# Roots of the layer norms on ScalarE in groups of tiles, projections ahead of turns, and expert bias products beside the first blocks

## The chip, the cores and the metric

One core of a Trainium2 chip runs the whole program in one launch. The metric is the device time of one execution in microseconds (us). TensorE is called PE in the rows, VectorE DVE, ScalarE ACT, GpSimd POOL and SyncE SP.

## What is computed

A stack of four levels over 64 sequences of 16 tokens, 192 wide, so 1024 tokens. Cut to what matters:

```python
h = tok(x, W, b, pos)                    # patches to tokens
h = h + L0_attn(layernorm(h))            # delays, one head
h = h + L0_ffn(layernorm(h))             # 8 linear experts, top 2, bias
h = h + L1_attn(layernorm(h))            # quantised, 12 heads
h = h + L1_ffn(layernorm(h))             # 4 T5 layers, two with 8 experts, own final norm
h = h + L2_attn(layernorm(h))            # rotary, 12 heads
h = h + L2_ffn(layernorm(h))             # 16 experts, top 2, bias of each expert
h = h + L3_attn(layernorm(h))            # partial rotary
h = h + L3_ffn(layernorm(h))             # 16 experts, top 8
```

`layernorm` subtracts the mean over the 192 columns and multiplies by `1/sqrt(variance + 1e-5)`. The bias of an expert layer is, for each token, the sum over experts of its weight times the expert's output bias.

## The kernel before, in words

The 1024 tokens are 8 tiles (`NT`) of 128 rows, and `h` stays in SBUF. The program is a row of stages (`..._phase`). A stage is one block in which each engine has an instruction stream of its own, written out by hand in loops; the streams wait for each other by counting semaphores, each engine in order, and a barrier of all engines stands between stages (`end_phase`, L181). Nothing reorders the work but the order of these loops. Inside a stage, a loop over steps `s` lets tile `t = s - d` go through its part `d` steps behind tile `s`.

Eight of the nine seams between sub-layers carry a layer norm that runs at the tail of the stage before it. Its parts for tile `t` are:

- VectorE: `bn_stats` and `bn_aggr` give mean and variance (`stats_behind`, L329), the second one step behind the first.
- POOL: `root` (L343) makes `rstd = (var + eps) ** -0.5` with a power, and `offset = -mean * rstd`, three instructions for one tile, each waiting for the one ahead of it.
- ScalarE: `normalise` (L355) writes `h * rstd + offset` to `k.rows`, 256 columns wide: 128 columns, and the other 64 twice, in two instructions; with a `dst` it writes 192 columns in one.
- TensorE: `turn_tile` (L370) transposes both halves of the 256 columns into a bank; ScalarE copies them to `xT` (`keep_tile`, L381); `tile_logits` (L390) multiplies by the router's weights.

The stages that the change touches: `embed_phase` (L221), `out_projection_phase` (L557, POOL adds the bias to `h`, L576), `linear_experts_phase` (L1494), `quant_projection_phase` (L1723, VectorE adds a bias to `h`, L1776), `quant_attention_phase` (L1806), `final_norm_phase` (L400; POOL takes the root of eight tiles' mean squares, L411, then adds to `h`, L416), `compact_attention_phase` (L635, for levels 2 and 3) and `expert_blocks_phase` (L1297, called for 8 experts twice and for 16 experts in level 2).

In `quant_attention_phase` ScalarE's stream has, in step `s`, first `normalise(s - 6)`, then the scores of tile `s` (L1885) and its share of spreading the attention over a block diagonal (L1892). VectorE does the rounding (L1915 to L1927), the context (L1936) and the add to `h` (L1941). POOL rounds the context in three instructions (L1963 to L1967), with `root(s - 5)` ahead of it in the same step.

In `compact_attention_phase` TensorE's step `s` holds scores of tile `s` (behind an idle product, L210, which only keeps TensorE at work), the output projection of tile `s - 4` (L688, one bank, so it waits for the add of the tile ahead, L744), the product with the values of tile `s - 2` (L816), logits of tile `s - 9` and the turn of tile `s - 8`, all turns through one bank.

In `expert_blocks_phase` tokens are sorted by expert into 31 blocks of 128 (23 with 8 experts). POOL fetches rows, weights and sends results by indirect DMA, four blocks ahead. TensorE turns a block's rows (L1368), multiplies (L1380, L1384), and a step later multiplies again (L1396). With `bias`, before the first block, TensorE makes eight products of 16 rows with the biases (L1404) in two banks in turn, and VectorE adds them to `h` (L1462) behind one add over all of `h` (L1459). At the end both rows of a token are brought back, weighted and added, and with `turn_sums` the norm and the turns follow, an idle product behind each turn.

## Time and profile before

| what | us |
|---|---|
| median of 3 runs | 1648.29 |
| lowest, highest | 1633.18, 4505.66 |
| the profiled execution | 1638.03 |
| its span in the profile | 1636.3 |
| embedding | 0 to 35.0 |
| output projection of level 0 | 85.0 to 108.8 |
| linear experts | 120.2 to 173.5 |
| quantised projection, quantised attention | 174.8 to 200.4, 201.3 to 253.1 |
| final norm | 1067.3 to 1088.0 |
| attention of level 2, of level 3 | 1121.4 to 1173.4, 1421.8 to 1475.0 |
| sparse experts of level 2 | 1202.7 to 1388.4 |

The profiled execution's time is 1.7 us above its span, which is what lies around the first and last instruction. The ends of stages are those of their last instruction; some 1.3 us of barrier follow each. A row of the timeline is start, length of the stretch in us, engine, line, operation, written tile <- read tiles, shapes and count; in brackets the idle time of the engine before it and the instruction that ended it. PEclk is the granted clock of TensorE as a share of 2.4 GHz.

### The profile page before, as it was taken

How to read it: one execution, taken by the hardware profiler on the slowest of the kernel's cores; microseconds unless marked ns; L12 is line 12 of the kernel's file. 1: busy time of each engine (PE TensorE's matmuls, PEld its weight loads, DVE VectorE, ACT ScalarE, POOL GpSimd, SP SyncE). 2: the span in 40 equal slices, each digit the busy share in tenths (PEclk: the TensorE clock that was granted, in tenths of full speed). 3: DMA queues.
4: the chain of work that ended last, by engine and by line, in shares of the span. 5: the costliest groups of instructions: out<-in, count | busy, mean ns of one | idle time of the engine just before them, and what ended most of it. 6: DMA issues, size and time to landing. Idle time of an engine off the chain costs nothing. (4 is left out here: it accounts for less than half of the span.)

```text
span 1636.3 us, 35722 instructions
## 1 busy us (share of the span) xinstructions
PE 1381.3 (84%) x14530; PEld 1046.4 (64%) x14530; DVE 591.0 (36%) x1577; ACT 508.8 (31%) x1387; POOL 574.1 (35%) x848
## 2 busy tenths in 40 slices
PE   6669657999998996899999899668569996995997
PEld 4354325888876895688877688624458884362756
DVE  2436562333334212333343411235431112443434
ACT  3330434343441111334343111234313334432120
POOL 2031654222322564323232256454326564350000
PEclk8769858999999998899999899879669998977999
DMA  3100202000003531200000353200044442100000
GB/s 128 39 10 5 97 1 88 3 2 2 12 15 142 176 124 62 90 2 2 2 15 12 150 190 102 91 26 5 27 184 137 165 159 77 37 3 29 30 29 19
DMA packets 40625, 101.96 MB, mean 62 GB/s; under 512 B 15952, under 2 KB 26324, under 8 KB 35344
## 3 DMA queue, kind: packets, MB, share of 16 engines
q0 software_dynamic: 18480, 58.56, 10.4%
q1 hardware_dynamic: 20256, 38.77, 7.0%
q8 instruction: 116, 1.90, 0.5%
q10 hardware_dynamic: 1728, 2.36, 0.5%
q14 instruction: 45, 0.37, 0.1%
HBM read 138.21 MB, written 11.50 MB: 91 GB/s over the span
## 5 line engine op out<-in xcount | busy, mean ns | idle before, releaser
L1396 PE MATMUL bank<-t_ew,t_hg 128*128 128x192 f32 x552 | 97.2, 327 | 0.0
L1433 ACT ACTIVATE t_hg<-bank 128x384 f32<-128x384 f32 x92 | 40.1, 488 | 178.0 <-PE bank L1384 110.1
L2300 POOL TENSOR_SCALAR t_rstd<-t_ssq 128x1 f32<-128x1 f32 x64 | 12.3, 192 | 219.9 <-ACT t_junk L2136 219.7
L1396 PEld LDWEIGHTS bank<-t_ew,t_hg 128*128 128x128 f32 x552 | 88.7, 190 | 0.2
L1708 DVE SCALAR_TENSOR_TENSOR h<-bank,cw,h 128x192 f32<-128x192 f32 x128 | 53.5, 418 | 87.4 <-PE bank L1631 70.3
L1429 ACT ACTIVATE l_hg<-bank,l_ew 128x128 f32<-128x128 f32 x186 | 51.4, 375 | 105.7 <-PE bank L1384 61.5
L1380 PE MATMUL bank<-t_xgT,t_ew 128*128 128x128 f32 x552 | 71.3, 279 | 13.0 <-DVE t_xgT L1474 11.6
L1282 POOL DMA_INDIRECT t_ew<-in_t_moe,source x46 | 47.5, 1033 | 91.0 <-DVE t_og L1483 45.7
L1380 PEld LDWEIGHTS bank<-t_xgT,t_ew 128*128 128x128 f32 x552 | 67.4, 193 | 16.8 <-DVE t_xgT L1474 14.3
L210 PE MATMUL bank<-blk,ident 128*128 128x384 f32 x96 | 49.3, 628 | 32.7 <-issue 19.7
L2057 PE MATMUL bank<-t_wo,t_ctx 128*128 128x192 f32 x384 | 71.0, 335 | 0.9 <-ACT t_ctx L2153 0.9
L366 ACT ACTIVATE rows<-h,offset,rstd 128x128 f32<-128x128 f32 (+1 forms) x96 | 43.7, 496 | 85.5 <-POOL offset L352 84.5
L1631 PEld LDWEIGHTS bank<-w,l_hT 128*128 128x128 f32 x384 | 62.1, 190 | 5.6 <-issue 4.5
L1396 PE MATMUL bank<-l_ew,l_hg 128*128 128x192 f32 x372 | 65.5, 326 | 0.0
L2057 PEld LDWEIGHTS bank<-t_wo,t_ctx 128*128 128x128 f32 x384 | 61.5, 190 | 6.0 <-issue 1.5
L1631 PE MATMUL bank<-w,l_hT 128*128 128x192 f32 x384 | 64.9, 329 | 0.1
L1473 DVE TENSOR_SCALAR t_xgT<-bank,ln2s 128x128 f32<-128x128 f32 x46 | 16.1, 350 | 129.9 <-PE bank L1368 83.2
L1613 PE MATMUL bank<-xT,w 128*128 128x512 f32 x96 | 48.5, 629 | 16.5 <-ACTq L1669 16.5
L2224 DVE TENSOR_SCALAR rows<-z,t_rstd 128x192 f32<-128x192 f32 x64 | 20.5, 320 | 114.6 <-POOL t_rstd L2301 114.6
L1396 PEld LDWEIGHTS bank<-l_ew,l_hg 128*128 128x128 f32 x372 | 59.7, 190 | 0.1
L1340 POOL DMA_INDIRECT rows_out<-t_og,dest x46 | 46.7, 1016 | 31.9 <-DVE t_og L1483 20.2
L1292 POOL DMA_INDIRECT t_xg<-rows_in,token x46 | 44.4, 965 | 36.4 <-DVE t_xgT L1474 19.7
(367 smaller groups left out, 3115.2 us busy)
## 6 DMA issues: line engine op xcount, KB each, us to landing
t_qkv<-in_t_wqkv SPq DMA_DIRECT2D x9, 576.0 KB
t_wo<-in_t_wo SPq DMA_DIRECT2D x8, 576.0 KB
w<-in_l_w SPq DMA_DIRECT2D x8, 576.0 KB, 4.1
wA<-in_t_wqkv SPq DMA_DIRECT2D x2, 1728.0 KB
patches<-in_patches SPq DMA_DIRECT2D x8, 384.0 KB, 5.7
rows_in<-rows SPq DMA_DIRECT2D x24, 128.0 KB, 1.7
t_wi<-in_t_wi SPq DMA_DIRECT2D x3, 576.0 KB
t_gg<-rows_out ACTq DMA_DIRECT2D x8, 192.0 KB, 4.4
```

The source lines that it names most:

```text
L210: pe.matmul(bank[:, 0:HPU * P], k.ident[:], k.blk[:].rearrange("p j q -> p (j q)"), start=True, stop=True)
L366: ins = act.activation(to, x, ACT.Identity, bias=k.offset[:, t:t + 1], scale=k.rstd[:, t:t + 1])
L1282: pool.indirect_dma_start(k.ew[i % W_SLOTS][:, 0:weights.shape[1]], None, weights, bass.IndirectOffsetOnAxis(ap=k.source[:, b:b + 1], axis=0),
L1292: pool.indirect_dma_start(k.xg[i % X_SLOTS][:], None, k.rows_in, bass.IndirectOffsetOnAxis(ap=k.token[:, b:b + 1], axis=0)).then_inc(k.x_l ...
L1340: pool.indirect_dma_start(k.rows_out, bass.IndirectOffsetOnAxis(ap=k.dest[:, own:own + 1], axis=0), k.og[b % O_SLOTS][:], None, bounds_che ...
L1380: pe.matmul(hidden(b, m % 2)[:, m // 2 * P:(m // 2 + 1) * P], w[:, m * P:(m + 1) * P], k.xgT[b % 2][:, 0, :], start=(m < 2), stop=False)
L1396: mm = pe.matmul(k.bank[6 + b % 2][:, 0:DIM], k.hg[b % 2][:, m, :], w[:, SPLIT + m * DIM:SPLIT + (m + 1) * DIM], start=(m == 0), stop=(m = ...
L1429: ins = act.activation(k.hg[b % 2][:, m, :], hidden(b, m % 2)[:, m // 2 * P:(m // 2 + 1) * P], func, bias=k.ew[b % W_SLOTS][:, EXPERT + m: ...
L1613: pe.matmul(pair[o], k.w1[s][:, (m + o) * P:(m + o + 1) * P], k.xTs[:, 0, cols], start=True, stop=False)
L1631: mm = pe.matmul(k.bank[4 + (u * banks + i) % 4][:, j * DIM:(j + 1) * DIM], k.hT[u % 2][:, m, t * P:(t + 1) * P], k.w2[s][:, m, :], start= ...
L1708: ins = dve.scalar_tensor_tensor(out, src, k.cw[:, tile, bass.ds(col, 1)], out, ALU.mult, ALU.add)
L2057: mm = pe.matmul(turn_bank[:, 0:DIM], buf.ctx[w % 2][:, m, :], layer(w).wo[:, m, :], start=(m == 0), stop=(m == FC - 1))
```

## The change

- Groups of tiles: (0, 1), (2, 3), (4, 5), (6), (7). ScalarE takes the square root of variance + eps of a whole group (`deviations`), VectorE the reciprocal, and the offset of the group (`norm_behind`), in six stages. In the embedding and the output projection VectorE normalises itself. In the attentions of levels 2 and 3 the root stays on POOL, by groups. In the final norm the root over all tiles is ScalarE's too.
- Statistics and aggregate of a tile stand in one step, where they were a step apart.
- Only 192 columns are normalised. A turn is two transposes and a product with the identity, which puts the other 64 columns on the second half of the partitions. Where the doubled rows are stored (level 2), ScalarE writes the last 64 again.
- More banks for turns: four in the final norm and the sparse tail, three in the output projection, one and then eight in the attentions.
- In the attentions, the output projections of tiles 6 and 7 stand ahead of the remaining turns and logits, and the logits of tiles 4 to 7 behind all turns.
- In the quantised attention a tile's add stands ahead of the context of a later tile, and the normalisation behind the score work. The quantised projection's bias adds go from VectorE to POOL, a stage earlier.
- Each of the eight bias products stands behind the turn of one of the first eight blocks, in the same bank, and VectorE adds it and the block's tile of `xn` behind the copy of the rows.

```diff
+GROUPS = ((0, 2), (2, 4), (4, 6), (6, 7), (7, 8))
...
+def norm_behind(k, dve, src, done, here=False):
...
+    def step(t):
+        if t < NT:
+            dve.wait_ge(done, t + 1)
+            dve.bn_stats(k.stats[:, t, :], src[:, t, :]).then_inc(k.seen, 1)
+        g = group_ending(t - 1)
+        if g is not None:
+            tiles = slice(*GROUPS[g])
+            dve.wait_ge(k.root_step, g + 1)
+            dve.reciprocal(k.rstd[:, tiles], k.std[:, tiles]).then_inc(k.inverted, 1)
+        if t < NT:
+            dve.wait_ge(k.seen, t + 1)
+            dve.bn_aggr(k.mv[:, t, :], k.stats[:, t, :]).then_inc(k.measured, 1)
+        if g is not None:
+            dve.wait_ge(k.inverted, g + 1)
+            if here:
+                for n in range(*GROUPS[g]):
+                    dve.tensor_scalar(k.xn[:, n, :], src[:, n, :], k.mv[:, n, 0:1], k.rstd[:, n:n + 1], ALU.subtract,
+                                      ALU.mult).then_inc(k.tile_normed, 1)
+            else:
+                dve.scalar_tensor_tensor(k.offset[:, tiles], k.mv[:, tiles, 0], -1.0, k.rstd[:, tiles], ALU.mult,
+                                         ALU.mult).then_inc(k.rooted, 1)
+
+    return step
+
...
+def deviations(k, act, t):
...
+    g = group_ending(t)
+    if g is not None:
+        tiles = slice(*GROUPS[g])
+        act.wait_ge(k.measured, t + 1)
+        act.activation(k.std[:, tiles], k.mv[:, tiles, 1], ACT.Sqrt, bias=k.eps[:, 0:1]).then_inc(k.root_step, 1)
...
+    pool.tensor_scalar(inv, k.mv[:, tiles, 1], 1.0, eps, ALU.mult, ALU.add).then_inc(k.root_step, 1)
+    pool.wait_ge(k.root_step, 2 * g + 1)
+    pool.tensor_tensor(inv, inv, k.power[:, tiles], ALU.pow).then_inc(k.root_step, 1)
+    pool.wait_ge(k.root_step, 2 * g + 2)
+    for n in range(*GROUPS[g]):
+        ins = pool.tensor_scalar(k.offset[:, n:n + 1], k.mv[:, n, 0:1], k.rstd[:, n:n + 1], -1.0, ALU.mult, ALU.mult)
+    ins.then_inc(k.rooted, 1)
...
+    act.wait_ge(k.rooted, GROUP_OF[t] + 1)
+    scales = dict(bias=k.offset[:, t:t + 1], scale=k.rstd[:, t:t + 1])
+    ins = act.activation(dst, src[:, t, :], ACT.Identity, **scales)
+    if doubled:
+        ins = act.activation(k.rows[:, t, DIM:ROW], src[:, t, P:DIM], ACT.Identity, **scales)
...
-    pe.transpose(bank[:, 0:P], k.rows[:, t, 0:P], k.ident[:])
-    pe.transpose(bank[:, P:2 * P], k.rows[:, t, P:ROW], k.ident[:]).then_inc(k.tile_turned, 1)
+    pe.transpose(bank[:, 0:P], k.xn[:, t, 0:P], k.ident[:])
+    pe.transpose(bank[0:REST, P:2 * P], k.xn[:, t, P:DIM], k.ident[:])
+    pe.matmul(bank[REST:P, P:2 * P], k.xn[:, t, P:DIM], k.ident[:], start=True, stop=True).then_inc(k.tile_turned, 1)
```

The embedding's ScalarE and the output projection's POOL:

```diff
-            for s in range(NT + 1):
-                if s < NT:
-                    normalise(k, act, k.h, s, k.xn[:, s, :])
-                t = s - 1
+            act.wait_ge(k.quant_a, 1)
+            for s in range(NT + 4):
+                deviations(k, act, s)
+                t = s - 4
...
         @block.gpsimd
         def _(pool):
-            for s in range(NT + 4):
-                if s < NT:
-                    pool.tensor_tensor(dst[:, s, :], dst[:, s, :], bias[:], ALU.add).then_inc(k.pool_step, 1)
-                if s >= 4:
```

The attentions of levels 2 and 3, TensorE:

```diff
+            for s in range(NT + 2):
                 t = s
...
+                if 4 <= s:
+                    output(s - 4)
...
                     value(pe, t, ptb[t % 2], o_banks(t)).then_inc(k.pv_done, 1)
-                t = s - 9
-                if 0 <= t < NT:
-                    if t == 0:
-                        pe.wait_ge(k.loaded, 16 * len(loads))
-                    tile_logits(k, pe, t, n_e)
-                t = s - 8
-                if 0 <= t < NT:
-                    turn_tile(k, pe, t, (7,))
+                if s == NT + 1:
+                    for t in range(NT - 2, NT):
+                        output(t)
+                if s >= 8:
+                    logits(s - 8)
+                if s >= 7:
+                    turn(s - 7)
+            logits(2)
+            turn(3)
+            logits(3)
+            for t in range(4, NT):
+                turn(t)
+            for t in range(4, NT):
+                logits(t)
```

The sparse experts, TensorE and VectorE:

```diff
+                if bias and 2 <= b < NT + 2:
+                    pe.wait_ge(k.acc_step, b - 1)
                 for c in range(2):
                     mm = pe.transpose(k.bank[b % 2][:, c * P:(c + 1) * P],
                                       k.xg[b % X_SLOTS][:, c * P:(c + 1) * P], k.ident[:])
+                if bias and b < NT:
+                    mm = pe.matmul(k.bank[b % 2][:, 2 * P:2 * P + DIM], k.cwT[0:n_e, b * P:(b + 1) * P], k.bout[0:n_e, :],
+                                   start=True, stop=True)
                 mm.then_inc(k.rows_turned, 1)
...
-            if bias:
-                for t in range(NT):
-                    if t >= 2:
-                        pe.wait_ge(k.acc_step, t - 1)
-                    pe.matmul(k.bank[6 + t % 2][:, 0:DIM], k.cwT[0:n_e, t * P:(t + 1) * P], k.bout[0:n_e, :],
-                              start=True, stop=True).then_inc(k.turned, 1)
-                pe.wait_ge(k.acc_step, NT)
             turn(0)
...
                         dve.tensor_copy(k.xgT[b % 2][:], turned).then_inc(k.rows_copied, 1)
+                    if bias and b < NT:
+                        link(dve.tensor_tensor(dst[:, b, :], k.bank[b % 2][:, 2 * P:2 * P + DIM], dst[:, b, :], ALU.add))
+                        dve.sem_inc(k.acc_step, 1)
+                        link(dve.tensor_tensor(dst[:, b, :], k.xn[:, b, :], dst[:, b, :], ALU.add))
```

The quantised attention, ScalarE and VectorE:

```diff
-            for s in range(NT + 6):
-                t = s - 6
-                if t >= 0:
-                    normalise(k, act, dst, t, k.z[:, t, :])
-                t = s
-                if t >= NT:
-                    continue
+            def behind(s):
+                deviations(k, act, s - 4)
+                if 0 <= s - 6 < NT:
+                    normalise(k, act, dst, s - 6, k.z[:, s - 6, :])
+
+            for t in range(NT):
...
                 ins.then_inc(k.pt_copied, 1)
+                behind(t)
+            for s in range(NT, NT + 6):
+                behind(s)
...
                     ins.then_inc(k.spread, 1)
+                t = s - 3
+                if t >= 0:
+                    dve.wait_ge(k.projected, t + 1)
+                    dve.tensor_tensor(dst[:, t, :], p_bank(t), dst[:, t, :], ALU.add).then_inc(k.added, 1)
                 t = s - 1
                 if 0 <= t < NT:
                     o = k.octx[t % 2]
...
-                t = s - 3
-                if t >= 0:
-                    dve.wait_ge(k.projected, t + 1)
-                    dve.tensor_tensor(dst[:, t, :], p_bank(t), dst[:, t, :], ALU.add).then_inc(k.added, 1)
-                    step(t)
+                if s >= 3:
+                    step(s - 3)
             step(NT)
```

ScalarE's rows in the quantised attention, from tile 5's spreading on (`z` is the normalised tile, `std` the root of a group). Before:

```order
L1892 ACTIVATE attb<-l_xr,unround 32x12x32 x2
L366 ACTIVATE z<-h,offset,rstd 128x192
L1885 ACTIVATE l_xb<-bank,qscale 128x384
L1892 ACTIVATE attb<-l_xr,unround 32x12x32 x2
L366 ACTIVATE z<-h,offset,rstd 128x192
L1885 ACTIVATE l_xb<-bank,qscale 128x384
L1892 ACTIVATE attb<-l_xr,unround 32x12x32 x2
L366 ACTIVATE z<-h,offset,rstd 128x192 x6
```

and with the change:

```order
L1960 ACTIVATE attb<-l_xr,unround 32x12x32 x2
L389 ACTIVATE std<-mv,eps 128x2
L1953 ACTIVATE l_xb<-bank,qscale 128x384
L1960 ACTIVATE attb<-l_xr,unround 32x12x32 x2
L416 ACTIVATE z<-h,offset,rstd 128x192
L1953 ACTIVATE l_xb<-bank,qscale 128x384
L1960 ACTIVATE attb<-l_xr,unround 32x12x32 x2
L389 ACTIVATE std<-mv,eps 128x2
L416 ACTIVATE z<-h,offset,rstd 128x192 x2
L389 ACTIVATE std<-mv,eps 128x2
L416 ACTIVATE z<-h,offset,rstd 128x192
L389 ACTIVATE std<-mv,eps 128x1
L416 ACTIVATE z<-h,offset,rstd 128x192
L389 ACTIVATE std<-mv,eps 128x1
L416 ACTIVATE z<-h,offset,rstd 128x192 x3
```

Each normalisation moved from ahead of a tile's scores to behind its spreading, and five roots came in.

TensorE's rows in the attention of level 3, from the value product of tile 7 on (L816, then L888; `wo` is the projection, `wr` the logits, `ident` the turns). Before:

```order
L816 MATMUL bank<-l_ptb,l_vx 32x32 x48
L396 MATMUL bank<-wr,xT 128x16
L397 MATMUL bank<-wr,xT 128x16
L377 MATMUL bank<-ident,rows 128x128
L378 MATMUL bank<-ident,rows 128x128
L688 MATMUL bank<-l_wo,l_ctxT 128x192 x2
L396 MATMUL bank<-wr,xT 128x16
L397 MATMUL bank<-wr,xT 128x16
L377 MATMUL bank<-ident,rows 128x128
L378 MATMUL bank<-ident,rows 128x128
L688 MATMUL bank<-l_wo,l_ctxT 128x192 x2
```

and with the change:

```order
L888 MATMUL bank<-l_ptb,l_vx 32x32 x48
L729 MATMUL bank<-l_wo,l_ctxT 128x192 x4
L450 MATMUL bank<-wr,xT 128x16
L451 MATMUL bank<-wr,xT 128x16
L430 MATMUL bank<-ident,rows 128x128
L431 MATMUL bank<-ident,rows 64x128
L432 MATMUL bank<-ident,rows 64x128
L450 MATMUL bank<-wr,xT 128x16
L451 MATMUL bank<-wr,xT 128x16
L430 MATMUL bank<-ident,rows 128x128
L431 MATMUL bank<-ident,rows 64x128
L432 MATMUL bank<-ident,rows 64x128
```

The last two projections stand together, ahead of the logits of tile 1, where each was followed by a tile's logits and turn.

TensorE's rows at the head of the sparse experts (`bout` are the biases, `xg` the rows of a block). Before:

```order
L1404 MATMUL bank<-bout,cwT 128x192 x8
L1368 MATMUL bank<-ident,l_xg 128x128 x2
L1380 MATMUL bank<-l_xgT,l_ew 128x128 x6
L1384 MATMUL bank<-l_xgT,l_ew 128x128 x6
L1368 MATMUL bank<-ident,l_xg 128x128 x2
```

and with the change:

```order
L1438 MATMUL bank<-ident,l_xg 128x128 x2
L1441 MATMUL bank<-bout,cwT 128x192
L1453 MATMUL bank<-l_xgT,l_ew 128x128 x6
L1457 MATMUL bank<-l_xgT,l_ew 128x128 x6
L1438 MATMUL bank<-ident,l_xg 128x128 x2
L1441 MATMUL bank<-bout,cwT 128x192
```

The run of eight became one behind each turn.

## Rows read from the trace of the kernel before

**Rows 1.** stretches: start:end, us, busy of PE, PEld, DVE, ACT, POOL, PEclk, DMA, GB/s

```profile
201.30:254.40 53.10, 23.31 (x224) 12.52 (x224) 29.00 (x76) 18.60 (x32) 31.74 (x52) 0.50 0.01 3
1202.60:1389.70 187.10, 162.67 (x1228) 143.96 (x1228) 34.75 (x95) 65.10 (x219) 98.10 (x118) 0.93 0.39 130
1421.70:1476.20 54.50, 48.62 (x1000) 33.28 (x1000) 23.35 (x64) 18.50 (x65) 25.42 (x48) 0.73 0.02 5
```

**Rows 2.** timeline, tail of the linear experts, POOL and ScalarE: start, us, instruction

```profile
168.06 0.19 POOL L348 TENSOR_SCALAR rstd<-mv 128x1 f32<-128x1 f32 x1 [4.35 <-DVE mv L338]
169.34 0.19 POOL L348 TENSOR_SCALAR rstd<-mv 128x1 f32<-128x1 f32 x1
...
173.14 0.38 ACT L1558 ACTIVATE xT<-bank 96x256 f32<-96x256 f32 x1 [0.49 <-PE bank L1515]
```

**Rows 3.** timeline, quantised attention, VectorE, ScalarE, POOL, TensorE

```profile
217.01 0.62 DVE L1915 SCALAR_TENSOR_TENSOR l_xr<-l_xb,rscal,near 128x384 f32<-128x384 f32 x1
220.63 0.60 DVE L1915 SCALAR_TENSOR_TENSOR l_xr<-l_xb,rscal,near 128x384 f32<-128x384 f32 x1
...
227.73 0.55 ACT L366 ACTIVATE z<-h,offset,rstd 128x192 f32<-128x192 f32 x1 [4.36 <-POOL offset L352]
...
243.38 1.07 POOL L1963 TENSOR_SCALAR octx<-octx 128x256 f32<-128x256 f32 x1
...
246.04 1.01 PE L1868 MATMUL bank<-l_wo,l_ctxT 128*128 128x192 f32 x2 [2.04 <-POOL l_ctxT L1967]
...
248.02 0.36 DVE L1941 TENSOR_TENSOR h<-bank,h 128x192 f32<-128x192 f32 x1 [3.28 <-PE bank L1869]
...
252.59 0.55 ACT L366 ACTIVATE z<-h,offset,rstd 128x192 f32<-128x192 f32 x1 [0.73 <-POOL offset L352]
```

**Rows 4.** timeline, embedding, TensorE, VectorE, ScalarE

```profile
16.57 0.31 PE L292 MATMUL bank<-ident,rows 128*128 128x128 f32 x1 [0.89 <-ACT rows L366]
...
27.54 0.36 DVE L322 TENSOR_TENSOR h<-bank,pos 128x192 f32<-128x192 f32 x1 [1.08 <-PE bank L284]
...
34.73 0.26 ACT L236 ACTIVATE xe<-bank 64x128 f32<-64x128 f32 x1
```

**Rows 5.** timeline, output projection, VectorE and TensorE

```profile
95.69 0.36 DVE L627 TENSOR_TENSOR h<-bank,h 128x192 f32<-128x192 f32 x1 [1.74 <-POOL h L576]
...
108.23 0.59 PE L397 MATMUL bank<-wr,xT 64*128 64x8 f32 x2
```

**Rows 6.** timeline, final norm, POOL and TensorE

```profile
1067.98 1.68 POOL L411 TENSOR_TENSOR std<-var,power 128x8 f32<-128x8 f32 x1 [2.76 <-DVE var L428]
...
1075.12 0.47 PE L377 MATMUL bank<-ident,rows 128*128 128x128 f32 x1 [24.27 <-ACT rows L366]
```

**Rows 7.** timeline, sparse experts of level 2, TensorE

```profile
1202.70 1.61 PE L1404 MATMUL bank<-bout,cwT 16*128 16x192 f32 x4 [5.60 <-PEq L183]
...
1209.90 0.69 PE L1368 MATMUL bank<-ident,l_xg 128*128 128x128 f32 x2 [0.45 <-DVE h L1462]
...
1218.68 2.12 PE L1396 MATMUL bank<-l_ew,l_hg 128*128 128x192 f32 x12
...
1223.20 2.12 PE L1396 MATMUL bank<-l_ew,l_hg 128*128 128x192 f32 x12
```

**Rows 8.** timeline, end of that stage, TensorE

```profile
1386.94 1.46 PE L210 MATMUL bank<-blk,ident 128*128 128x384 f32 x4
```

**Rows 9.** timeline, tails of the attentions of levels 2 and 3, TensorE

```profile
1154.80 0.32 PE L688 MATMUL bank<-l_wo,l_ctxT 96*128 96x192 f32 x1 [1.63 <-issue]
...
1461.53 1.48 PE L688 MATMUL bank<-l_wo,l_ctxT 96*128 96x192 f32 x4
...
1474.35 0.61 PE L397 MATMUL bank<-wr,xT 64*128 64x16 f32 x2
```

**Rows 10.** timeline, ScalarE, a table load at the head of a stage

```profile
254.45 1.28 ACT L2136 ACT_TABLE_LOAD   x1 [1.31 <-PEq L183]
255.75 0.36 ACT L2136 ACTIVATE t_junk<-z 128x192 f32<-128x192 f32 x1
```

229 lines of the change are left out of this document (109 added, 120 removed).

## The prediction

> **What bounds the kernel now.** I read the busy time and granted clock of the stages first, then the groups by line, then the timeline engine by engine at the seams between stages, because the chain that ended last only covers the final stage, which the change doesn't touch. The kernel is a row of stages between barriers, so a stage is worth what its own last instruction is late by. The table of stages says which have slack: in the quantised attention no engine is busy more than 31.7 of 53.1 us and the granted clock is 0.50, so it is bound by waits; in the last attention TensorE is busy 48.6 of 54.5 us at 0.73; in the sparse expert stage 162.7 of 187.1 [rows 1]. The waits in question are those for the root: each of 64 tiles (8 in each of eight stages) has three POOL instructions of its own, among them the power, and one root starts 1.28 us behind the other (168.06, 169.34) [rows 2]. Where eight tiles arrive faster than that, the tail of the stage is POOL's.
>
> **The change part by part.** Times are against the profiled execution: span 1636.3 us, 1638.0 us on the clock of the runs, so 1.7 lie around it. The median of the three runs is 1648.3, but with two at 1633.2 and 1648.3 I hold 1638.0 for the centre.
>
> Quantised attention. ScalarE stood 4.36 us before tile 0's normalisation, which is ahead of tile 6's scores in its program, and as long again before tile 1's: POOL reached the root only behind a whole context step. VectorE's tile steps start 3.62 apart until then (217.01, 220.63) [rows 3]. Now ScalarE takes a root for two tiles behind its own spreading, and the normalisation stands behind the tile's score work, so both stalls go. VectorE gets earlier statistics, a reciprocal and an offset, 0.15 to 0.2 each, 1.1 in the three tile steps that matter. Step 7 ends near 220.6 + 3 x 3.6 + 1.1 = 232.6. The end of the stage is now VectorE's new order: the add of tile 5 before the context of tile 7, so that context leaves at about 235.1; POOL takes 2.66 to pass it on (243.38 to 246.04), the projection 1.98 (246.04 to 248.02) [rows 3], which is 239.8; statistics, root, reciprocal and offset 1.2 to 1.4, three normalisations of 0.45 in a row, end 242.5. Before it was 252.59 + 0.55 = 253.1. Gain 10.5; bounds 8 (one more step of 3.6 lost in part) and 12 (no reorder cost).
>
> Embedding. TensorE waited 0.89 for tile 0's normalisation and needn't now. From the last add (27.54) to the end (34.99) there are 7.45 us [rows 4]. Now statistics, root and aggregate take 1.2, and ScalarE then works off the copies of five tiles at 0.65 each: 4.4. Gain 0.9 + 3.0 = 3.9; bounds 2 and 5.
>
> Output projection. POOL's bias add is queued behind a root, and VectorE waits 1.74 for it; the same happens for the next two tiles through TensorE. The stage ends at 108.8 [rows 5]. With the eight adds in one run (0.6 each from 85.0) there is no such wait. VectorE now normalises itself and becomes the bound: add, statistics, aggregate, half a reciprocal, normalisation, 1.25 a tile from tile 3 at 93, 99.5 at the last. Then turns and logits of the last three tiles, 1.4 each warm and 1.85 cold: 104.3. Gain 4.5; bounds 2 and 6.
>
> Linear experts. TensorE bounds the loop and stays so; the tail takes three roots in a row from 168.06 and ends at 173.5 [rows 2]. Now tiles 6 and 7 alone are left behind the last add, with roots of 0.2: 170.9. Gain 2.6; bounds 1.5 and 3.5. The bias adds, gone from VectorE's quantised projection to POOL here, are 0.6 each beside free time; the projection ends with POOL anyway, gain 0.4, bounds 0 and 1.
>
> Final norm. The power of eight columns took 1.68; a root and a reciprocal do it in 1.1 from the barrier, the 1.28 of a table load being most of it. TensorE starts at 1075.12 with the first turn [rows 6] and would start at 1073.3. Its work grows, since a turn is now three products and not two: 0.4 a tile cold, 0.2 warm. Gain 1.4; bounds -0.5 and 3.
>
> Sparse experts, head. TensorE and VectorE spend 1202.70 to 1209.90, 7.2 us, on eight bias products before the first block turns [rows 7]. Now each stands behind the turn of one of the first eight blocks: 0.33 warm, 0.75 the first. A block takes 4.53 (1218.68, 1223.20 [rows 7]), and VectorE's two more adds (0.8) lie under TensorE's second product. 7.2 - 0.75 - 7 x 0.33 = 4.1; some blocks wait for fetched rows anyway and may swallow part, so I take 4.3; bounds 1 (the first blocks run cold twice as long) and 7.
>
> Sparse experts, tail. It ends at 1388.4 [rows 8]. The first turn would come 0.75 earlier, but TensorE's idle products bound the rest, and the third product of a turn costs it 0.4 a tile cold. Gain 0.5; bounds -1 and 2.
>
> Attentions of levels 2 and 3. Roots stay on POOL for pairs, and cost 1.4 a pair. The last projection ran from 1461.53 and would run from about 1459.9. But it is now followed by seven logits and six turns instead of six and five: 7 x 1.07 + 6 x 0.95 + 0.9 of waits = 14.1, where 12.2 were spent before until 1474.96 [rows 9]. Nothing is won there while the clock is at 1.2 GHz; at 2.4 GHz the same work is 8. In level 2 TensorE stood 1.63 without work shown before 1154.80 [rows 9], which may have cost the clock; I take 3.0 for level 2 and 0.8 for level 3; bounds for both together -2 and 11.
>
> Table loads. Six more: three at the head of a stage, where the first use is over a microsecond off, three before a root. The row shows 1.28 and the next ScalarE instruction 0.02 behind it [rows 10]; where it stands in mid-stream (output projection, sparse tail) the root's inputs are not ready 0.9 us of it. I count 0.5 in all, which the terms above hold already. The Trainium skill ("ScalarE: Activation LUTs", What ACT_TABLE_LOAD costs) says that a switch is 1.28 us of load and 1.38 us of drain. The load agrees with the row; no drain shows here, but these rows have nothing in flight before them. By the page the two mid-stream switches and the final norm would cost 1.4 each more, and the sum would be 4 less.
>
> Sum: 10.5 + 3.9 + 4.5 + 2.6 + 0.4 + 1.4 + 4.3 + 0.5 + 3.8 = 31.9, no overlap since each lies in its own stage. 1638.0 - 31.9 = 1606, or 1.95%. A measurement of this kernel tells about 2%, 32.8 us, from no change, so the forecast stands on that line, a hair below.
>
> **The rivals.**
> A. The clock carries the attentions. If TensorE keeps 2.4 GHz through the tails of both, they end 4 to 5 us earlier each than taken, and the embedding and output tails lie at their upper bound: 1606 - 9 - 2 = 1595. For it: TensorE is denser with the projections back to back. Against it: it was at 1.2 GHz in both tails before, busy four fifths of the time [rows 9].
> B. The tails are given back. VectorE becomes the bound where it normalises, every root is a round trip VectorE, ScalarE, VectorE behind in-order queues, and drains are paid at the switches. Each of the six tails gives half its gain: 0.5 x (3.9 + 4.5 + 2.6 + 1.4) = 6, the quantised attention is at its lower bound, 2.5, the attentions give nothing, 3.8, and switches 2: 1606 + 14 = 1620. For it: the added waits stand in queues, ScalarE's root of a pair before the copies of earlier tiles in the embedding and the output projection.
> C. Slower. The sparse experts become bound by their fetches. Four blocks are in flight, a block is 4.53 us, and some waits of 1.8 us show already. If the bias work on VectorE delays each block's copy and so POOL's next fetch, the 27 fetched blocks all wait 1.8: 49 us, less the 27.6 of the other stages: 1638 + 21 = 1659. It decides from the point where a fetch takes longer than three blocks. Against it: the DMA engines are busy 0.39 in that stage [rows 1], and only eight blocks carry the extra work.
> D. The change doesn't do what it says: an in-order queue locks the new order into the old one in the quantised attention (the root of a pair waits for an aggregate that waits for the score work). Then 10.5 is lost: 1616. Against it: the aggregate of tile 1 stands a whole step before the root that reads it.
>
> **How the numbers follow.** Forecast (gain 25 to 40) 0.55; A 0.13; B 0.19; C 0.03; D 0.10. The runs of before spread over 15 us, which lies on both sides of each. From 1592 to 1628 leaves out half of A's far side, C and a little of B: about 0.15 to 0.2. Faster by over 2% needs 32.8: half of the forecast's 0.55 and all of A: 0.40. Slower by over 2% is part of C alone: 0.02. Within 2%: 0.58.
>
> **What would show it.** Right: no idle time of ScalarE over 1 us before a normalisation in the quantised attention, and that stage about 42 us and not 53; the first block's turn within 1 us of the barrier; first blocks 4.9 apart; the output projection some 19 us long. The tail of the level 3 attention after its last projection 14 us long at the low clock would confirm that it wins nothing, 9 that A holds. Wrong: ScalarE waiting long for an aggregate, VectorE for a root; 1.4 us of nothing before a table load; block distances over 6 for most blocks.

## The result and the profile after

The changed kernel takes 1634.5 us (median of 20 executions, 1623.1 to 1644.9), the kernel before in the same comparison 1644.2 (20 executions, 1632.3 to 1653.0 but for one of 4505.7). The ratio is 0.9946, with a 95% interval of 0.9925 to 0.9967: a gain of half a per cent, some 9 us, where I had forecast 31.9. A second comparison (chip 11; twelve executions of the changed kernel, 29 of the one before) gives 0.997 (0.9937 to 1.0002). Neither is a difference of 2%, and 1606 with its range of 1592 to 1628 was wrong. Some 6 us of the distance from 1606 to 1634.5 lie in the base alone: I took 1638.0 for the kernel before, and its median is 1644.2.

The stages tell more than the sum. These are rows of the changed kernel's profile by stretches (length; busy us and count of TensorE, its weight loads, VectorE, ScalarE, POOL; the granted clock as a share of full; DMA share; GB/s), in the order: quantised attention, the first and the second pair stage of the T5 layers, attention of level 2, sparse experts of level 2, attention of level 3.

```profile
195.00:237.30 42.30, 23.01 (x224) 12.35 (x224) 30.96 (x86) 19.44 (x37) 23.73 (x28) 0.51 0.01 3
237.30:487.30 250.00, 242.33 (x3806) 196.55 (x3806) 90.00 (x203) 98.25 (x300) 72.23 (x133) 0.97 0.06 21
645.80:897.40 251.60, 240.43 (x3806) 195.02 (x3806) 89.99 (x203) 98.24 (x300) 72.39 (x133) 0.98 0.06 21
1112.60:1168.80 56.20, 49.68 (x1016) 31.81 (x1016) 24.89 (x64) 18.23 (x65) 23.60 (x42) 0.81 0.08 24
1196.90:1380.90 184.00, 163.75 (x1244) 143.91 (x1244) 36.78 (x112) 64.78 (x217) 89.91 (x94) 0.96 0.39 132
1412.90:1469.20 56.30, 51.61 (x1016) 33.44 (x1016) 24.89 (x64) 15.70 (x57) 23.58 (x42) 0.75 0.02 5
```

The first, fifth and sixth answer to [rows 1] (53.1, 187.1, 54.5). The quantised attention won what was forecast. The last attention got longer by 1.8 us, with 16 matmuls more and 3 us more of TensorE's time. And the two T5 stages, which the change doesn't touch, have the same 3806 matmuls as before but are longer: in the first profile of before they were 245.2 and 248.8 us.

Every stage from its start to the next one's start, before minus after (a gain is positive), for the first profiles of both kernels (the one of before is that of the prediction) and for a second pair from the second comparison. Lines are rounded each for itself:

| stages | predicted | first pair | second pair |
|---|---|---|---|
| quantised attention | 10.5 | 10.9 | 10.8 |
| embedding | 3.9 | 2.6 | 3.1 |
| output projection | 4.5 | 3.6 | 2.5 |
| linear experts | 2.6 | 2.8 | 2.9 |
| quantised projection | 0.4 | -0.6 | -0.5 |
| final norm | 1.4 | 0.6 | -0.1 |
| sparse experts of level 2, head and tail | 4.8 | 3.1 | -0.1 |
| attentions of levels 2 and 3 | 3.8 | -4.6 | -11.6 |
| the two T5 pair stages | 0 | -7.8 | -11.0 |
| level 0 attention | 0 | -1.6 | -0.1 |
| all others | 0 | -2.9 | 1.1 |
| sum | 31.9 | 6.0 | -3.0 |

So some 20 us came in the four stages whose waits went, where 21.5 were forecast. Most of it was paid back in other stages. One profile has a luck of its own: the second one of before was faster (1609.6 us) than all 29 other executions of that kernel in its comparison (1612.6 to 1639.3), so the second column flatters the kernel before, and the ratios, not these sums, say what the change is worth. The table is for finding the places. One line of it is not the change's: the 1.6 us of the level 0 attention are 3.4 us at 1.2 GHz at the head of that stage, which the other three profiles don't have.

Two places in the trace show what was paid. The first is TensorE's timeline in the tail of the level 2 attention, behind its last projection: one turn (lines 430, 431, 432) and the first product of the next.

```profile
1160.64 0.48 PE L430 MATMUL bank<-ident,rows 128*128 128x128 f32 x1
1160.91 0.42 PE L431 MATMUL bank<-ident,rows 128*64 128x128 f32 x1
1161.26 0.69 PE L432 MATMUL bank<-ident,rows 128*64 128x128 f32 x2
1161.88 0.48 PE L430 MATMUL bank<-ident,rows 128*128 128x128 f32 x1
```

A turn takes 1.24 us (1160.64 to 1161.88). The third product is one line but "x2": it has two matmul records (two passes, I call them), where a transpose has one. The tail, from the end of the last projection to the last logits, is 15.74 us long in both attentions; before it was 11.94.

The second is in the untouched T5 stage, TensorE's timeline in the products of the probabilities with the values (line 2177), 96 tiny ones in a row:

```profile
451.95 0.88 PE L2162 MATMUL bank<-t_kx,t_qT 128*32 128x64 f32 x48
452.76 1.14 PE L2177 MATMUL bank<-t_ptb,t_v 32*64 32x32 f32 x92
455.03 0.30 PE L2177 MATMUL bank<-t_ptb,t_v 32*64 32x32 f32 x4 [1.14 <-issue]
```

After 92 of them TensorE stands for 1.14 us "on issue", in the middle of a row of equal products that wait for nothing. I numbered TensorE's instructions in the trace (weight loads, matmuls and those of its sequencer): this place is number 8642, the other such place of the stage (1792 or 7 times 256 earlier) number 6850, and in the second T5 stage, a second pass over the same code, numbers 16692 and 18484, again 1792 apart. The page lists a queue that carries TensorE's program (packets, MB, share of the DMA engines' time):

```profile
q8 instruction: 117, 1.92, 0.5%
```

117 loads of 16 KB for 29,936 instructions, 256 to a load. The instructions that the change adds ahead of this stage (32 in the output projection, less one) moved every later one, and so moved which of them is the first of a load. The Trainium skill ("Runtime: NRT & Kernel Launch", Instruction fetch mechanics) says that an engine's program comes in blocks of 16 KiB, 256 instructions, and that crossing into the next is mostly hidden. The trace agrees on the block and its size; that it is hidden holds at most boundaries here, and not at these.

The times of these loads are in the trace, and they settle what TensorE waits for. The load ahead of number 8642 landed at 453.60 and TensorE went on at 455.03, 1.43 us later; ahead of number 6850 the two are 400.86 and 402.12, 1.26 apart. In the fourteen profiles of this study, the T5 stages and the attentions of levels 2 and 3 hold 77 pauses of 0.45 us or more at such a number, and 76 of them end 1.2 to 1.6 us after a load has landed; of the boundaries that TensorE passed without a pause (0.15 us or less), 9 in 100 lie in such a place by chance.

The kernel before has them too. Its boundaries have the same numbers, but other products stand there (line 2021, 128x128): 0.41 us at 8642 and at 18484 in its first profile, 0.28 at 6850 in its second. And [rows 9] shows one that I read without knowing it: the 1.63 us "on issue" before 1154.80 in the attention of level 2 are at number 23348, which is 23604 less 256; that load landed at 1153.33, 1.47 us before TensorE went on.

### The profile page after: what moved, and what is told of

The parts are those of the page before. It is cut to its first block and busy times, and to the rows that moved or that the text cites. A ratio compares the mean times of both kernels' runs of the same rounds, so it can differ in the third digit from the quotient of the medians.

```text
span 1630.2 us, 35793 instructions
## 1 busy us (share of the span) xinstructions
PE 1398.5 (86%) x14610; PEld 1054.0 (65%) x14610; DVE 606.6 (37%) x1644; ACT 503.9 (31%) x1376; POOL 524.6 (32%) x699
## 5 line engine op out<-in xcount | busy, mean ns | idle before, releaser
L1453 PE MATMUL bank<-t_xgT,t_ew 128*128 128x128 f32 x552 | 72.7, 283 | 14.3 <-DVE t_xgT L1534 13.3
L1453 PEld LDWEIGHTS bank<-t_xgT,t_ew 128*128 128x128 f32 x552 | 68.3, 196 | 18.6 <-DVE t_xgT L1534 16.7
L211 PE MATMUL bank<-blk,ident 128*128 128x384 f32 x96 | 46.9, 600 | 28.7 <-issue 18.2
L1469 PEld LDWEIGHTS bank<-l_ew,l_hg 128*128 128x128 f32 x372 | 59.7, 190 | 1.5 <-issue 1.4
L1413 POOL DMA_INDIRECT rows_out<-t_og,dest x46 | 46.7, 1016 | 33.5 <-DVE t_og L1547 21.9
L1453 PE MATMUL bank<-l_xgT,l_ew 128*128 128x128 f32 x372 | 48.5, 281 | 7.7 <-DVE l_xgT L1537 7.7
```

The lines of the kernel that those rows point to most:

```text
L211: pe.matmul(bank[:, 0:HPU * P], k.ident[:], k.blk[:].rearrange("p j q -> p (j q)"), start=True, stop=True)
L1413: pool.indirect_dma_start(k.rows_out, bass.IndirectOffsetOnAxis(ap=k.dest[:, own:own + 1], axis=0), k.og[b % O_SLOTS][:], None, bounds_che ...
L1453: pe.matmul(hidden(b, m % 2)[:, m // 2 * P:(m // 2 + 1) * P], w[:, m * P:(m + 1) * P], k.xgT[b % 2][:, 0, :], start=(m < 2), stop=False)
L1469: mm = pe.matmul(k.bank[6 + b % 2][:, 0:DIM], k.hg[b % 2][:, m, :], w[:, SPLIT + m * DIM:SPLIT + (m + 1) * DIM], start=(m == 0), stop=(m = ...
```

## The experiments

The theory: (1) the third product of a turn costs two passes, in every turn behind the final norm, the attentions and the sparse experts; (2) more instructions on TensorE's queue move its program loads to places where they are late, and a late load can take the clock with it; (3) the rest is as predicted. Rivals: chance of single executions, the time at which the clock rises above all; the attentions' new order; the parts other than the quantised attention give nothing for reasons of their own.

### Both kernels again

No edit; the kernel before, once, and the changed kernel in twelve executions.

> The kernel before, unchanged, once more, for its stages. My theory: the stage lengths of the first profile are properties of the program, so the first relative-position (T5) stage is again 243.9 + 1 us from its first to its last instruction, the second 247.4, the attentions of levels 2 and 3 53.4 and 54.5 from start to the router's start, and TensorE has no stall inside a row of products at 0.8 us or over in the T5 stages. Rival (chance): the T5 stages differ from the first profile by 3 us or more.

> The changed kernel, unchanged, once more. My theory: it is some 0.5% faster than the kernel before (ratio 0.993 to 0.997); the T5 stages are again 4.9 and 2.9 us longer than before's, with the same two stalls of TensorE inside the products on the value tiles (0.3 and 1.1 us, 89 and 59 products in), and the attentions of levels 2 and 3 take 56.2 us each. Rival (chance): the T5 stages come out at before's 243.9 and 247.4.

Measured: the T5 stages came to 245.3 and 247.6 us in the kernel before, without a stall of 0.3 us inside a row, and to 249.9 and 253.9 in the changed one, with stalls at numbers 6850 and 8642 (0.42 and 0.86 us) and at 16692 and 18484 (0.59 and 0.82). The places are the program's; the sizes vary. Chance as the only cause of the T5 loss is out, as the stalls are there again; but the lengths have a share of it: the clock rose 6.6 us into the second T5 stage in the kernel before and 16.7 us into it in the changed one, and, as the runs below show, the same code has it at either. But I was wrong on the attentions of the kernel before: 50.1 and 49.8 us, not 53.4 and 54.5.

```profile
1108.80:1158.90 50.10, 43.65 (x1000) 28.46 (x1000) 23.30 (x64) 18.24 (x65) 25.34 (x48) 0.84 0.09 26
1187.40:1365.50 178.10, 161.41 (x1228) 144.30 (x1228) 35.08 (x95) 64.95 (x219) 97.71 (x117) 0.93 0.41 136
1397.60:1447.50 49.90, 43.12 (x1000) 28.61 (x1000) 23.36 (x65) 18.24 (x65) 25.36 (x48) 0.85 0.02 5
```

Against [rows 1]: the same attention of level 3 at a granted clock of 0.85 in place of 0.73 is 4.6 us shorter, and the changed kernel has 57.9 and 53.7 here. But this is the fastest execution of the kernel before. Over six profiles with this very code in the attentions they take 49.8 to 56.1 us, 53.4 in the mean, so the row that I built the term on (54.5) was an ordinary one, and a single pair tells little. The sparse experts took 178.1 us and not 187.1, again with the same code. In the first profile a block took 5.1 to 6.1 us ten times, in pairs every fourth or fifth block, here nearly all take 4.53. The changed kernel has such blocks in its first profile too (up to 6.03 us) and none in its second; these pauses come and go between comparisons and executions, and nothing I ran tells their cause.

### Moving TensorE's program, first try: waits

In the delay stage, where TensorE does nothing:

```diff
+        @block.tensor
+        def _(pe):
+            for _ in range(448):
+                pe.wait_ge(k.evacuated_a, 1)
```

> The changed kernel with 226 instructions more on TensorE's queue, all waits that are already met, in the delay stage where TensorE has nothing to do. They move every later TensorE instruction by 226 places, which with the 31 that the change added by the T5 stages makes about one whole load of the program (16 KB, 256 instructions). My theory: the stalls of TensorE come at fixed places of its instruction stream (those of the two profiles all stand at the same number modulo 256 within a pass), where the next 16 KB of program have not arrived; so the T5 stages lose their stalls of 1.1 us and the clock drop behind the first, and come back to some 245.5 and 247.5 us (before 243.9 and 247.4, plus the later rise of the clock in the first). 5 to 6 us less than the changed kernel, ratio to before 0.990 to 0.992. Rival (the stalls belong to what the engines compute there, or to chance): the T5 stages stay at 248.8 and 250.2, the ratio at 0.995.

Measured: ratio 1.0007 (0.9972 to 1.0043), slower than the changed kernel alone. By stretches, the delay stage and the first T5 stage:

```profile
32.50:60.30 27.80, 0.00 (x0) 0.00 (x0) 12.34 (x10) 11.09 (x10) 0.00 (x0) 0.50 0.17 45
243.40:488.60 245.20, 238.57 (x3806) 193.35 (x3806) 90.00 (x203) 98.37 (x300) 72.23 (x133) 0.99 0.06 21
```

The T5 stage is at 245.2 as forecast, the length it had before the change; one stall of 0.38 us is left in it. Part of that is the clock, which rose 4.3 us into the stage here and 9.3 in the changed kernel's run. The 448 waits are 224 instructions in the trace, two waits in each, and a met one takes TensorE 0.11 us, so they took 24 us and made the delay stage 10.1 us longer. And TensorE stood 2.32 us in the attention of level 2, at number 23604: its loads had moved, too. The second T5 stage, at 252.7, wasn't what I expected: its clock rose only 13.3 us in, and stalls of 0.32 and 0.43 us are left.

### The same with tiny transposes

```diff
+            for _ in range(112):
+                pe.transpose(k.bank[7][0:32, 0:32], k.ident[0:32, 0:32], k.ident[0:32, 0:32])
```

> The changed kernel with 225 TensorE instructions more in the delay stage, now as 112 tiny transposes of 32x32 in place of waits (the 226 waits took 10.1 us of their own in the run before and hid what they gave). My theory: the delay stage stays at 17.7 us within 1; the first T5 stage falls from 249.9 to 245 to 246 with no stall of 0.8 us or more inside a row of products, the second keeps the later rise of the clock at its head and loses 1 to 2 us; in the attention of level 2 a stall of about 2 us remains, at another product. In all 3 to 6 us under the changed kernel, ratio to before 0.991 to 0.995. Rival (places in the program don't matter): 0.997, T5 stages at 250 and 252.

Measured: 0.9954 (0.9928 to 0.998). The stretches: delay stage, both T5 stages, attention of level 2.

```profile
33.90:51.60 17.70, 6.13 (x112) 6.00 (x112) 12.34 (x10) 11.09 (x10) 0.00 (x0) 0.50 0.28 70
237.90:484.40 246.50, 240.33 (x3806) 194.98 (x3806) 89.98 (x203) 98.28 (x300) 72.02 (x133) 0.98 0.06 21
636.60:886.60 250.00, 239.45 (x3806) 194.61 (x3806) 89.98 (x203) 98.29 (x300) 72.16 (x133) 0.98 0.06 21
1095.60:1155.70 60.10, 53.62 (x1016) 34.39 (x1016) 24.89 (x64) 18.24 (x65) 23.54 (x42) 0.74 0.07 22
```

The shift is free now, and the T5 stages win 3.3 and 3.9 us on the changed kernel's 249.9 and 253.9. Of these the 3.3 are a clean comparison: in both profiles the clock rises 9.4 us into the first stage, and the one difference is two stalls of together 1.28 us and 3.4 us at 1.2 GHz behind them. The 3.9 are not, since the clock rises 6.9 us into the second stage here and 16.7 there; one stall of 0.68 us is left in it (number 18228). The attention of level 2 is at 60.1, with a stall of 2.05 us at number 23604. What the shift wins in one stage it loses in the next, unless it is chosen for both. By the ratio alone it is not to be told from the changed kernel (0.9946 and 0.997).

### Before's attentions in the changed kernel

The functions of before for the attentions of levels 2 and 3 (order, single roots, two-product turns); all else changed.

> The changed kernel with the attentions of levels 2 and 3 as before: roots of single tiles, projections behind the turns, turns of two products on doubled rows. My theory: these two stages go back from 56.2 and 56.3 us to 53.4 and 54.5, which is 4.6 us less, ratio to before 0.990 to 0.993; the sparse experts and the hidden stage stay within 1 us. Rival 1 (the attentions lost by chance of the clock or of program loads, not by their new order): they stay at 55 or more. Rival 2 (other stages take it back): the attentions fall but the sum does not.

Measured: 0.9938 (0.9909 to 0.9968), where the changed kernel in the same comparison had 0.997. The stages were 54.8 and 54.0 us, after 57.9 and 53.7. The level 3 one holds a stall of 1.71 us at number 28468, which the kernel before doesn't have there. So the attentions may be some 0.3% of the loss, but the intervals overlap, and the ratios don't show it.

### Two-product turns, order kept

```diff
-    pe.transpose(bank[0:REST, P:2 * P], k.xn[:, t, P:DIM], k.ident[:])
-    pe.matmul(bank[REST:P, P:2 * P], k.xn[:, t, P:DIM], k.ident[:], start=True, stop=True).then_inc(k.tile_turned, 1)
+    pe.transpose(bank[:, P:2 * P], k.rows[:, t, P:ROW], k.ident[:]).then_inc(k.tile_turned, 1)
...
-                normalise(k, act, dst, t, k.xn[:, t, :], doubled=keep)
+                normalise(k, act, dst, t, k.xn[:, t, :], doubled=True)
```

in the final norm, the attentions of levels 2 and 3 and the sparse experts' tail.

> The changed kernel with its order kept, but every turn in the final norm, in the attentions of levels 2 and 3 and in the tail of the sparse experts made of two products on rows that ScalarE has doubled, as before, in place of three, the third of which TensorE runs in two passes (0.35 us each at 1.2 GHz). My theory: a turn at the low clock falls from 1.24 to 0.7 us; the attentions of levels 2 and 3 fall by 2 to 5 us each from 57.9 and 53.7, the final norm and the tail by 1 to 2 each; ratio to before 0.988 to 0.993. Rival 1 (the attentions lose by the order, with projections ahead of all turns, and by the clock that falls in it): less than 1.5 us each, the tail stays 16 us long. Rival 2 (ScalarE becomes the bound with a second part for every tile): final norm and tail grow.

Measured: 0.9885 (0.9842 to 0.9929), a median of 1603.7 us where the kernel with tiny transposes above, in the same comparison, has 1613.9. TensorE's timeline in the same tail as above:

```profile
1149.59 0.42 PE L688 MATMUL bank<-ident,rows 128*128 128x128 f32 x1
1149.81 0.42 PE L689 MATMUL bank<-ident,rows 128*128 128x128 f32 x1
1150.02 0.42 PE L688 MATMUL bank<-ident,rows 128*128 128x128 f32 x1
```

A turn is 0.43 us at the low clock where it was 1.24, and the tail is 11.14 us and not 15.74. The final norm fell by 3.1 us (22.2 to 19.1) and the sparse experts by 3.8 (178.2 to 174.5). The tail of 16 us of rival 1 and the growing stages of rival 2 are out: the order alone doesn't make the tail long, and ScalarE has room for the second part. But the attentions as a whole are 55.0 and 54.4, the first 2.9 shorter and the second not shorter at all, where I expected 2 to 5 each; each has a stall at a program load again, 2.31 and 2.02 us.

### The mirror: the third product alone, in the kernel before

```diff
-    pe.transpose(bank[:, P:2 * P], k.rows[:, t, P:ROW], k.ident[:]).then_inc(k.tile_turned, 1)
+    pe.transpose(bank[0:REST, P:2 * P], k.rows[:, t, P:DIM], k.ident[:])
+    pe.matmul(bank[REST:P, P:2 * P], k.rows[:, t, P:DIM], k.ident[:], start=True, stop=True).then_inc(k.tile_turned, 1)
```

> The kernel before with one thing alone: a turn is three products (the second half of a tile turned twice, once as a product into the lower partitions) where it was two; the rows are still doubled by ScalarE as before, and nothing else is touched. It is the mirror of turn2all. My theory: the third product is two passes, 0.57 us a tile at the low clock; the tails of the attentions behind the last projection go from 11.9 to 15 to 16.5 us, the final norm and the sparse experts' tail grow by 2 to 4 us each, the output projection by 0 to 3; in all 10 to 15 us slower, ratio to before 1.006 to 1.010, the mirror of the 0.85% that turn2all gives back. Rival (turn2all gained by chance of the clock or by fewer program loads): 1.000 to 1.003, tails of 12 to 13 us.

Measured: 1.0149 (1.0109 to 1.0189), 23 us slower by the medians (1645.6 and 1622.6), more than I expected. The stretches: output projection, both T5 stages, attention of level 2; and the timeline of the first T5 stage in the values' products.

```profile
84.20:113.10 28.90, 24.78 (x112) 18.31 (x112) 5.67 (x24) 12.11 (x32) 12.49 (x32) 0.73 0.00 1
257.00:505.20 248.20, 240.34 (x3806) 194.96 (x3806) 89.95 (x203) 98.26 (x300) 72.22 (x133) 0.98 0.06 21
658.10:911.50 253.40, 242.27 (x3806) 196.56 (x3806) 89.94 (x203) 98.28 (x300) 72.36 (x133) 0.97 0.06 21
1117.50:1177.20 59.70, 53.17 (x1016) 34.26 (x1016) 23.52 (x64) 18.27 (x65) 25.45 (x48) 0.73 0.07 22
```

```profile
471.16 1.14 PE L2112 MATMUL bank<-t_ptb,t_v 32*64 32x32 f32 x92
472.89 0.30 PE L2112 MATMUL bank<-t_ptb,t_v 32*64 32x32 f32 x4 [0.59 <-issue]
```

The eight third products of the output projection are 32 more TensorE instructions (a weight load and a matmul for each pass, and two passes), the same 32 as in the changed kernel. With them alone the stalls are at 6850, 8642, 16692 and 18484 inside the values' products, after the 92nd of 96 at number 8642 as above, and larger than the kernel before has them at these numbers (0.5 to 1.0 us); the T5 stages are at 248.2 and 253.4, though the clock of the second, which rose 13.1 us in, has its share. This joins the two halves of the theory: one cause, a third product per turn, costs its passes where it stands and program loads where it doesn't. The attentions went to 59.7 and 59.8 (tails 15.04, where the same order with two products has 11.94), the output projection up by 3.8, final norm and sparse experts by only 1.0 and 1.7.

### Idle products ahead of the T5 stage

In both profiles of the changed kernel the clock rose 9.3 to 9.4 us into the first T5 stage, in both of the kernel before 4.3 to 4.4. I took that for the change's doing.

```diff
+            idle_products(pe, k, k.bank[0], 5)
```

behind the last projection of the quantised attention.

> The changed kernel with five idle products (0.7 us each at 1.2 GHz) behind TensorE's last projection of the quantised attention, where it otherwise has nothing to do for 4 us until the barrier. My theory: the first T5 stage loses 1.6 us because the clock there rises 9.3 us after the stage's start and not 4.1 as before; with TensorE busy up to the barrier the clock rises within 5 us of the start, the stage is 1 to 2 us shorter than 249.9, and the quantised attention's own 42.3 us stay within 0.3. Ratio to before 0.995 to 0.998 (about 0.1% under the changed kernel's, less than a ratio tells; the stage decides). Rival (the rise has nothing to do with the idle time before): the clock rises 9 us in again and the stage stays at 249.9.

Measured: 0.9976 (0.9946 to 1.0006). The two stages:

```profile
195.50:240.10 44.60, 28.02 (x234) 14.95 (x234) 30.95 (x86) 19.43 (x37) 23.69 (x28) 0.54 0.01 3
240.10:487.50 247.40, 238.40 (x3806) 193.76 (x3806) 89.99 (x203) 98.16 (x300) 72.01 (x133) 0.99 0.06 21
```

The clock was up before the T5 stage began, which won 2.5 us with the stalls as before (0.40 and 1.05). But the five products took 5.0 us and not 3.5 (each is two records again) and ended behind the normalisations, and the quantised attention grew by 2.3. The lever is real and was worth nothing as I pulled it. Nor is the late rise the change's: the kernels with before's attentions and with two-product turns run the same TensorE code up to here and have the rise at 4.3 and 5.1 us.

### Two-product turns and a shift chosen for them

From the traces I worked out, for each shift, how long TensorE takes over each stretch of 256 instructions in the T5 stages and the new attentions. At 227 more, none is shorter than 2.5 us. The edit is the kernel with two-product turns and 113 tiny transposes in the delay stage. Beside it ran the same with the attentions as before the change and a shift of its own.

> The kernel of turn2all (two products a turn behind the final norm, the new attentions and the sparse experts) with 227 TensorE instructions more in the delay stage, 113 tiny transposes. At 227 places on, no stretch of 256 instructions of the T5 stages or of the new attentions is issued in under 2.5 us (worked out from the start times in the traces so far). My theory: the stalls inside rows of products, 2.8 us in the T5 stages and 4.3 in the two attentions of turn2all, fall under 1 us in all, the clock stays up in more of the tails, the first T5 stage is 245 to 246, the attentions 50 to 53 each; 5 to 9 us less than turn2all, ratio to before 0.981 to 0.986. Rival (the stalls were other things' and come back at new places): 0.9885 again, stalls of 2 us in the attentions.

> The same with the attentions of levels 2 and 3 as before the change (projections behind turns, root for each tile), and the shift chosen for them (169 in the delay stage, 32 in the final norm). It compares the two orders of these attentions with two-product turns in both and few stalls in either. My theory: the new order gives and takes nothing much; the two stages come to 50 to 53 us in both kernels and differ by less than 1.5 each. Rival 1 (the order ahead of the turns is a loss, since the tail runs at the low clock): this kernel's attentions are 3 us or more shorter each. Rival 2 (the order is a gain of 2 us each once the turns are cheap): they are longer by that.

Measured: 0.9824 (0.9787 to 0.9862), a median of 1598.8 against 1622.9, the fastest kernel of this study; its interval lies on both sides of a gain of 2%. Its T5 stages and attentions:

```profile
241.00:486.30 245.30, 238.93 (x3806) 193.37 (x3806) 89.91 (x203) 98.27 (x300) 71.99 (x133) 0.99 0.06 21
641.40:889.90 248.50, 238.79 (x3806) 193.35 (x3806) 89.91 (x203) 98.26 (x300) 72.16 (x133) 0.99 0.06 21
1096.00:1150.30 54.30, 47.79 (x1000) 32.73 (x1000) 24.91 (x64) 18.33 (x65) 23.56 (x42) 0.75 0.08 25
1386.70:1440.70 54.00, 48.14 (x1000) 32.68 (x1000) 24.87 (x64) 18.22 (x65) 23.54 (x42) 0.75 0.02 5
```

Inside rows of products of the T5 stages no stall over 0.2 us is left, in the attentions one of 0.27. But between rows two are left there, ahead of a turn in level 2 (number 23604) and at a projection in level 3 (1.00 us, number 28468); they end 1.4 and 1.5 us after a load has landed. The first:

```profile
1131.02 0.45 PE L688 MATMUL bank<-ident,rows 128*128 128x128 f32 x1 [1.85 <-issue]
```

The 256 instructions ahead of it had taken 3.4 us, so the 2.5 us that I chose the shift by are no bound. The attentions stay at 54, with these stalls and with the clock low for their last 20 and 17 us; my 50 to 53 was wrong. The kernel with before's attentions had 0.9893 (0.9849 to 0.9936) and 55.7 and 56.2 us, but its shift was chosen badly (stalls of 2.12 and 1.56 us are in it). So which order is better for these attentions isn't settled: the new one is not a loss of 3 us, and no gain of it is shown. The two kernels' medians in this comparison, 1598.8 and 1606.7, differ by more than the attentions do.

### One part alone: the quantised attention

Kernel before, with only that stage's new code.

> The kernel before with one part of the change alone: the quantised attention with ScalarE's roots for groups behind its spreading and with VectorE's new order. TensorE's program keeps its length, so that the places of its program loads stay as before. My theory: that stage goes from 53.1 to 42.3 us as in the whole change, the first T5 stage keeps 245 us (no stall of over 0.3 us inside a row of products) or pays 1 to 2 us for a later rise of the clock, and all else stays; 9 to 11 us less, ratio to before 0.993 to 0.995. So this part alone gives as much as the whole change (0.995 and 0.997). Rival (the other parts give their share too and this one less than the stage shows): 0.997 or above.

Measured: 0.9946 (0.9927 to 0.9965), the ratio that the whole change had in the first comparison (0.997 in the second). Its stage and the T5 stage behind it:

```profile
201.10:244.80 43.70, 23.31 (x224) 12.52 (x224) 30.94 (x86) 20.71 (x38) 23.69 (x28) 0.50 0.01 3
244.80:491.10 246.30, 239.84 (x3806) 194.79 (x3806) 89.92 (x203) 98.26 (x300) 72.01 (x133) 0.99 0.06 21
```

43.7 and not 42.3: ScalarE has one instruction more (x38), since the table load falls into this stage (in the whole change it has been done ahead). So all other parts of the change together came to nothing that these intervals can tell. TensorE's program is untouched here, yet the second T5 stage took 252.5 us from barrier to barrier, 3.4 to 4.5 more than in the kernel before's two profiles: its clock rose 13.2 us in. Not all of the T5 stages' loss in the table is thus the change's.

### One part alone: the experts' bias

Kernel before, with only the bias products moved beside the first eight blocks.

> The kernel before with the part on the sparse experts' bias alone: no eight products ahead, one beside the turn of each of the first eight blocks. My theory: the first output copy comes 4.5 us earlier than before's 18.2 to 18.6 after the stage's start, five of the distances behind it are 5.23 and not 4.53 (a product of fp32 is two passes of 0.35 us) and the whole stage is 1.0 to 1.5 us shorter, not 4.3 as predicted; ratio to before 0.998 to 1.000, no difference that can be told. Rival (the distances in the profiles of the changed kernel came from something else, the tail's three-product turns or the places of program loads): distances of 4.9 or 4.53 and a stage 4 us shorter.

Measured: 1.0007 (0.9988 to 1.0026). VectorE's first two output copies of the sparse experts:

```profile
1213.23 0.36 DVE L1479 COPY l_og<-bank 128x192 f32<-128x192 f32 x1 [3.02 <-PE bank L1401]
1218.11 0.36 DVE L1479 COPY l_og<-bank 128x192 f32<-128x192 f32 x1 [1.01 <-PE bank L1401]
```

The stage starts at 1194.0, so the first copy comes 19.2 us in, later than before's 18.2 to 18.6 and not 4.5 earlier. The following distances are 4.9, 5.2, 5.2, 5.2 and 5.2 us as forecast. The rival is out. What went wrong is the clock at the head:

```profile
1194.00:1212.20 18.20, 17.01 (x70) 13.71 (x71) 3.14 (x9) 4.59 (x13) 0.94 (x1) 0.50 0.15 51
```

It was at 0.50, which is 1.2 GHz, for 18 us, with TensorE 17.0 us busy. In the changed kernel's first profile it rose 5.5 us in and the first copy came at 13.2. Where the clock rises late, real blocks run through the low clock in place of the short bias products. It is no trait of this kernel alone: of the ten profiles with the bias work beside the blocks, eight have the rise 5.4 to 7.5 us in and the first copy at 13.2 to 14.2; this one and the one with idle products have the rise at 18.3 and 18.1 and the copy at 19.2 and 18.7. In the four with before's head it rises 11.3 to 12.7 us in. So the part wins 4 to 5 us at the head in most profiles and lost 0.6 in this one, and a single profile doesn't price it; what decides isn't shown.

## Why the prediction was wrong

The forecast's mechanism for the main term held. The quantised attention is 42.3 us, forecast "about 42": the score work follows without ScalarE's stall, and the last add starts 38.4 us into the stage (233.40 less 195.0), where before it was 46.7 (248.02 [rows 3] less 201.3). With it rival D is out. One sign that I had named for being wrong did come and meant nothing: ScalarE waits up to 2.2 us for an aggregate in the tail, but the adds set the pace there. The linear experts are right within 0.3 us. Embedding and output projection gave 2.6 to 3.1 and 2.5 to 3.6, inside their bounds of 2 to 5 and 2 to 6, but 1 to 2 us below the values taken; where the clock is low in the output projection's last 7 us (both profiles with two-product turns and the new order) only 0.7 to 0.8 is left of the latter. The table loads are right as I took them: in mid-stream of the output projection ScalarE ends a copy, loads, and takes the root with nothing between.

```profile
88.26 0.38 ACT L661 ACTIVATE l_ctxT<-bank 96x256 f32<-96x256 f32 x1 [1.33 <-PE bank L636]
88.66 1.28 ACT L389 ACT_TABLE_LOAD   x1
89.95 0.30 ACT L389 ACTIVATE std<-mv,eps 128x2 f32<-128x2 f32 x1
```

The drain of 1.38 us of the Trainium skill ("ScalarE: Activation LUTs", What ACT_TABLE_LOAD costs) doesn't show here: 0.02 us stand between the copy and the load.

The step that failed is the price of the turn: "a turn is now three products and not two: 0.4 a tile cold, 0.2 warm". Measured against the tiles of the tails, a turn went from 0.43 (0.48 in [rows 9]'s own tails) to 1.24 us at the low clock, 0.8 more. The tails of the attentions, forecast at 14.1 us with six turns at 0.95, were 15.7, for which six turns at 1.24 account, and not the 11.9 of before; with the third product gone they are 11.1. In two terms the price, too low as it was, wasn't even added: for the final norm I took 1.8 us of earlier start less 0.4, where eight turns at my own 0.2 are 1.6, and for the sparse tail a gain of 0.5, where eight at 0.4 are 3.2. They came to 0.6 and -0.1 for the norm and to a loss of 0.3 and 1.3 for the tail. The trace of before had the price, in a stage I read for another reason: the embedding turns its tiles with the same kind of product, here at the low clock.

```profile
30.16 0.47 PE L292 MATMUL bank<-ident,rows 128*128 128x128 f32 x1 [1.82 <-ACT rows L366]
30.56 0.69 PE L293 MATMUL bank<-ident,rows 128*64 128x128 f32 x2
```

The bias product fell to the same error. [rows 7] has four matmuls in 1.61 us for two products at the low clock. I took 0.33 a product at the high one; the changed kernel's row there shows two matmuls and 0.59:

```profile
1217.82 0.59 PE L1441 MATMUL bank<-bout,cwT 16*128 16x192 f32 x2
```

Five of the distances between blocks grew by 0.70 (5.23 and not 4.53), where I had 4.9 in mind. In the second pair, with the first copy 4.4 us earlier (18.6 to 14.2) and 3.5 given back over the distances, 0.9 of the 4.3 is left, and the tail took that back.

The second failure is a term I didn't have: what a change does to stages that it doesn't touch. "No overlap since each lies in its own stage" was the sentence. The T5 stages lost 7.8 and 11.0 us in the two pairs. For the first stage the parts are shown: the stalls at program loads, with the clock that fell behind them, are 3.3 us (249.9 against 246.6 with the loads moved and the same late rise), and the later rise of the clock at the head is 1 to 2 (4.3 and 9.4 us in). The stalls are the program's and the rise is the execution's. The fall of the clock within a stage goes with the stalls: in the T5 stages of all fourteen profiles it fell fifteen times for some 3.4 us, each time 0.2 to 2.0 us behind the end of a pause at a program load, and never elsewhere; behind rather more than half of these pauses it didn't fall. In the second stage the rise, 16.7 us in against 6.6, is about half of the second pair's loss by an estimate: 9.4 us at the low clock at the head cost 2.5 in the first stage (249.9 against 247.4 with idle products ahead), so 10 more cost some 3. All profiles together, from barrier to barrier:

| TensorE's program in the T5 stages | profiles | first stage, mean | second stage, mean |
|---|---|---|---|
| as before the change | 4 | 245.2 to 247.1, 246.0 | 248.0 to 252.5, 250.2 |
| third product in the output projection, not shifted | 6 | 246.1 to 250.1, 248.4 | 251.4 to 257.4, 253.5 |
| the same, shifted | 4 | 245.3 to 246.6, 245.7 | 248.9 to 253.1, 250.6 |

So the change costs these two stages 5 to 6 us in the mean, and not 7.8 or 11.0, and a shift gives it back.

The third is the 3.0 us that I took for level 2, on the ground that a gap of 1.63 us would go and the clock stay up. The gap was a program load; the changed kernel has two there (0.84 and 1.31 us, numbers 23348 and 23604), and the clock was low for the last 17.6 us of the stage, where it was for 18.2 before. With the clock these stages vary by 6 us for the same code, so single pairs mislead here as well:

| code of the attentions of levels 2 and 3 | profiles | us | mean |
|---|---|---|---|
| before's order, two products a turn | 6 | 49.8 to 56.1 | 53.4 |
| before's order, three products | 1 | 59.7, 59.7 | 59.7 |
| new order, three products | 5 | 52.8 to 60.0 | 56.7 |
| new order, two products | 2 | 54.0 to 55.0 | 54.4 |

By the means the changed kernel loses 3.3 us a stage here, 2.3 of it by the third product.

Rivals: A didn't come, since the clock stays low in both tails (only in the second profile's level 3 was a part of it at the high one, and it took 13.6 us). B's 1620 was nearest to the number, but not for its reasons: the tails with new roots kept most of their gain, and what was given back went to the third product. C is out: behind the first eight the blocks stand 4.53 us apart in the second pair, and in the first pair both kernels have the same longer ones. The forecast of 1.95% isn't far from what the change gives once its turns have two products and its loads are placed: 1.76%. That doesn't make it right, as the changed kernel has neither.

## What to carry to other kernels

Count passes, not products: before pricing a matmul that replaces a transpose, find a row of the same kind in the trace and look at its count beside its time. Where an engine issues hundreds of tiny instructions in a row, adding instructions anywhere ahead of them can move a program load into that row; compare the untouched stages first when a gain goes missing, and number the engine's instructions at their "issue" stalls. Take a stage's length from several executions before building a term on it or reading a loss from it: the same attention code took 49.8 to 56.1 us, and the fastest execution misleads as much as a slow one. And add each price that you name to every term that pays it.

## What was unexpected of the hardware

- TensorE's program loads of 16 KB can be late: stalls of 0.3 to 1.1 us in the T5 stages, up to 2.3 in the attentions, at the same numbers of the stream for the same program. Where the 256 instructions ahead had taken 1.6 and 2.0 us, a stall was there in all six profiles; where they had taken 3 to 3.5 us, in some. TensorE went on 1.2 to 1.6 us after a load had landed in 76 of 77 pauses. In the longest stalls of the attentions (1.0 us and more at 23348 and 23604) that load had itself started only 2.0 to 3.4 us behind the boundary before it, in those at 6850 and 8642 within 1.3; why it starts late in the attentions is open.
- In the T5 stages the granted clock fell fifteen times in fourteen profiles, always within 2.0 us of the end of such a pause (0.25 us and longer), and never in a T5 stage without one.
- 448 waits that are already met are 224 TensorE instructions and take 24 us, 0.11 each; 112 transposes of 32x32 in their place were 6.1 us of work, hidden in a stage of 17.7 us.
- The same head of the sparse experts' stage saw the clock rise 5.5 us after its start in one execution and 18 in another, with TensorE 17.0 of 18.2 us busy in the latter; that moved the first output by 6 us.
- Pauses of 1.8 us every fourth or fifth block of the experts cost one profile of the kernel before 9 us in one stage and were absent from its second. Their cause is open.
